# The last unit of cross-attention rows in a fused attention and expert kernel: another order of sums, residuals, keys and stores

## The reference

```
x = x + xattn(layernorm(x), ctx, ctx)      # 8 heads, queries and keys normalized per head, softmax(5 * q.k)
n = layernorm(x)
logits = n @ Wg + bg                       # 4 experts
top-2 experts of each row, softmax of their logits -> probs
for each expert i:
    the 512 rows with the highest probs of those assigned
    out[those rows] += (gelu(n[rows] @ W1[i]) @ W2[i]) * prob
x = x + out
```

## Time and profile before

| what | us |
|---|---|
| median of 3 runs (lowest to highest) | 597.75 (597.01 to 599.29) |
| the profiled execution, its own time | 598.06 |
| span of its profile | 596.2 |
| PE busy in the span | 567.0 (95%) |
| DVE busy | 342.2 (57%) |
| ACT busy | 292.4 (49%) |
| POOL busy | 184.5 (31%) |

### The profile page before, as it was taken

One profiled execution on the slowest core, in us unless ns is written; L12 is line 12 of the kernel. 1 busy time (PEld: TensorE's weight loads), 2 busy tenths in 40 slices (PEclk: granted clock), 3 DMA queues, 4 the chain that ended last, 5 costly groups with the idle time before them and its releaser, 6 DMA issues.

```text
span 596.2 us, 8893 instructions
## 1 busy us (share of the span) xinstructions
PE 567.0 (95%) x2933; PEld 403.8 (68%) x2936; DVE 342.2 (57%) x682; ACT 292.4 (49%) x451; POOL 184.5 (31%) x146
## 2 busy tenths in 40 slices
PE   8999999999997558999999999999999999999995
PEld 4445555545544325888888888888888888888884
DVE  5779999999979683534355434355534255424212
ACT  3989888788885323333334333334333334333320
POOL 8466565565632425000401500401500401500002
PEclk9999999999998859999999999999999999999998
DMA  4523433433222224422522542522542522542001
GB/s 157 195 74 124 142 110 108 142 107 107 91 90 89 100 95 141 123 90 71 187 97 88 186 149 70 180 100 86 169 168 70 181 101 81 172 170 70 1 0 71
DMA packets 49004, 67.91 MB, mean 114 GB/s; under 512 B 10960, under 2 KB 27472, under 8 KB 48976
## 3 DMA queue, kind: packets, MB, share of 16 engines
q1 hardware_dynamic: 45136, 54.97, 28.2%
q0 software_dynamic: 3840, 12.59, 6.3%
HBM read 54.77 MB, written 12.64 MB: 113 GB/s over the span
## 4 chain that ended last, share of the span: by engine, by line
PE 80%; DVE 6%; issue 5%; ACT 3%; POOL 3%; DMA 1%; POOLq 0%; DVEq 0%; ACTq 0%; SPq 0%
PE two L1541 29%; PE four L1576 10%; PE four L1574 10%; PE four L1575 10%; PE two L1364 6%; PE four L1354 5%; PE two L1379 2%; POOL rnorm L526 2%; PE four L1406 1%; PE bank_t L1399 1%; DVE junk L1126 1%; PE bank_m L1326 1%; PE bank_t L1333 1%; DVE half_sum L928 1%; PE bank_m L1341 1%
## 5 line engine op out<-in xcount | busy, mean ns | idle before, releaser
L824 ACT ACTIVATE h_f<-two 128x512 f32<-128x512 f32 x64 | 38.3, 598 | 218.8 <-PE two L1541 218.8
L1294 DVE TENSOR_TENSOR h_lo<-h_f,h_hi 128x512 fp32r<-128x512 f32 x62 | 42.7, 689 | 110.7 <-ACT h_hi L825 110.7
L1541 PE MATMUL two<-xt_hi,w_hi 128*128 (+1 forms) x256 | 101.3, 396 | 0.7 <-issue 0.7
L1541 PE MATMUL two<-xt_hi,w_lo 128*128 (+1 forms) x256 | 99.9, 390 | 0.0
L1541 PE MATMUL two<-xt_lo,w_hi 128*128 (+1 forms) x256 | 99.2, 389 | 0.0
L1576 PE MATMUL four<-w_hi,h_lo 128*128 128x512 f32 x248 | 96.5, 389 | 0.0
L1574 PE MATMUL four<-w_hi,h_hi 128*128 128x512 f32 x248 | 96.5, 389 | 0.0
L1575 PE MATMUL four<-w_lo,h_hi 128*128 128x512 f32 x248 | 96.5, 389 | 0.0
L714 ACT ACTIVATE prob<-four,rnorm 128x512 f32<-128x512 f32 x128 | 77.8, 704 | 18.3 <-POOL rnorm L526 15.1
L1263 DVE TENSOR_TENSOR w_lo<-raw,w_hi 128x2048 fp32r<-128x2048 f32 x30 | 68.7, 2290 | 23.4 <-ACT w_hi L747 23.4
L526 POOL TENSOR_TENSOR rnorm<-ss_max,power 128x8 f32<-128x8 f32 x32 | 59.2, 1851 | 42.4 <-DVE ss_max L877 28.0
(11 more groups left out here) (195 smaller groups left out, 772.2 us busy)
## 6 DMA issues: line engine op xcount, KB each, us to landing
raw<-in_L_ffn_W SPq DMA_DIRECT2D x64, 512.0 KB, 4.3
x_all<-in_x SPq DMA_DIRECT2D x16, 256.0 KB, 2.9
c_sb<-in_ctx SPq DMA_DIRECT2D x16, 256.0 KB, 3.2
out<-x_all SPq DMA_DIRECT2D x16, 256.0 KB, 2.4
x2n_dram<-x2n SPq DMA_DIRECT2D x16, 256.0 KB, 3.0
p_inv<-inv_dram SPq DMA_DIRECT2D x30, 128.0 KB, 2.9
few<-p_sum SPq DMA_DIRECT2D x60, 2.0 KB, 1.8
cst<-in_consts SPq DMA_DIRECT2D x1, 423.5 KB, 4.7
```

Of the source, the lines that this page charges most:

```text
L824: nc.scalar.activation(h_f[m % 2][:, :], z_ps[m % 2][:, :], ACT.Gelu)
L1294: nc.vector.tensor_tensor(h_lo[n][:, :], h_f[m % 2][:, :], h_hi[n][:, :].bitcast(F32), ALU.subtract).then_inc(h_split, 1)
L1541: return nc.tensor.matmul(z[:, :], w_part[c][:, w], x_k, start=start, stop=stop)
```

## The change

It does the following.

- SP: behind unit 12, unit 14's few sums are taken right behind unit 13's inverse; the stores of unit 12's and 13's x2 and x2n come behind them, three of these four also behind unit 14's inverse.
- VectorE, last unit: both pairs of half sums come before the inversion of unit 14's few sums; the first pair comes before the normalization of unit 12; the statistics of unit 13 come last. Behind `invert_sums`: residual 14 (from GpSimd), logits 12, x2n 13, statistics 14, residual 15, statistics 15, x2n 14, logits 13, x2n 15, then the first 12 units' keys, logits 14 and 15, the last keys and their copy, and only then the first count.
- GpSimd: no residual; the first two weight remainders wait for the last sums instead of the last x2n and come ahead of the last two `finish`.
- TensorE: in the last unit the full-width sums come in two parts, each as soon as its half sums are there, behind the transposes and ahead of the last weighted values and the router product of unit 12; behind it, other idle products, the transposes of unit 15 ahead of the router product of 14, and all keys transposed at the end, the first 12 units' in three parts.
- ScalarE: the rows of 14 and 15 are taken before the keys, unit 15's into a new tile `x2n_last`; the copy of the first keys is three copies of four units.

```diff
@@ sync @@
-            for u in ((end - 1, 0), (end - 1, 1), (end, 0)):
-                pass_unit(u, 3, None, None)
+            pass_unit((end - 1, 0), 3, None, None)
+            take_few((end - 1, 1))
+            store_x2n((end - 2, 1))
+            spread_inverse((end - 1, 1))
+            take_few((end, 0))
+            store_x2((end - 1, 0))
+            spread_inverse((end, 0))
+            store_x2n((end - 1, 0))
+            store_x2((end - 1, 1))
             store_x2n((end - 1, 1))
             for u in ((end, 0), (end, 1)):
                 store_x2(u)
@@ gpsimd @@
-            residual((UNITS // 2 - 1, 0))
+            pool.wait_ge(sums_ready, UNITS)
+            for q in range(2):
+                first_low(0, q)
             finish((UNITS // 2 - 1, 0))
             finish((UNITS // 2 - 1, 1))
-            pool.wait_ge(x2n_done, UNITS)
-            for q in range(2):
-                first_low(0, q)
-            pool.wait_ge(key_done, 2)
+            pool.wait_ge(late_keys, 1)
             first_low(0, 2)
@@ scalar @@
             take_x2t((UNITS // 2 - 2, 1))
-
-
+            take_x2t((UNITS // 2 - 1, 0), bank_m)
+            take_x2t((UNITS // 2 - 1, 1), rows=x2n_last)
             act.wait_ge(key_set, 1)
-            nc.scalar.activation(key_w[:, 0:EARLY, :, :], key[:, 0:EARLY, :].unsqueeze(3)
-                                 .broadcast_to([P, EARLY, E, WAYS]), ACT.Copy).then_inc(key_done, 1)
-            take_x2t((UNITS // 2 - 1, 0), bank_m)
-            take_x2t((UNITS // 2 - 1, 1))
+            for t in range(0, EARLY, 4):
+                nc.scalar.activation(key_w[:, t:t + 4, :, :], key[:, t:t + 4, :].unsqueeze(3)
+                                     .broadcast_to([P, 4, E, WAYS]), ACT.Copy).then_inc(key_done, 1)
...
-            act.wait_ge(key_t, 1)
+            act.wait_ge(key_t, 2)
             count_signs(0)
@@ vector, unit @@
-                if behind > 2:
+                if behind > 2 and ahead:
                     normalize_x2(before(before(before(u))), behind > 4)
-                if not ahead:
-                    residual(before(before(u)))
-                    statistics_x2(before(before(u)))
...
                 for h in range(2):
                     half_sums(u, 0, h, behind > 0)
-                if behind:
+                if not ahead:
+                    normalize_x2(before(before(before(u))), True)
+                    residual(before(before(u)))
+                if behind and ahead:
                     invert_few(before(u))
...
-                if not ahead:
-                    normalize_x2(before(before(u)), True)
                 for h in range(2):
                     half_sums(u, 1, h, behind > 0)
                 if not ahead:
-                    dve.wait_ge(logit_done, EARLY)
-                    keys_of(0, EARLY)
-                if behind > 2:
+                    invert_few(before(u))
+                if behind > 2 and ahead:
                     take_logits(before(before(before(u))))
-                if behind > 1 and ahead:
-                    residual(before(before(u)))
+                if behind > 1:
+                    if ahead:
+                        residual(before(before(u)))
                     statistics_x2(before(before(u)))
@@ vector, behind the units @@
             invert_sums(end)
+            residual(before(end))
+            take_logits(before(before(before(end))))
+            normalize_x2(before(before(end)), True)
             statistics_x2(before(end))
             residual(end, 1)
+            statistics_x2(end)
             normalize_x2(before(end), True)
             take_logits(before(before(end)))
-            statistics_x2(end)
             normalize_x2(end, True)
+            dve.wait_ge(logit_done, EARLY)
+            keys_of(0, EARLY)
             take_logits(before(end), bank_m)
+            take_logits(end)
             early = EARLY * P
-            dve.wait_ge(key_t, 1)
+            dve.wait_ge(logit_done, UNITS)
+            keys_of(EARLY, UNITS)
+            dve.wait_ge(key_set, 2)
+            nc.vector.tensor_copy(key_w[:, EARLY:, :, :], key[:, EARLY:, :].unsqueeze(3)
+                                  .broadcast_to([P, UNITS - EARLY, E, WAYS])).then_inc(late_keys, 1)
+            dve.wait_ge(key_t, 3)
             dve.wait_ge(thr_done, 1)
...
             put(nc.vector.scalar_tensor_tensor(rest0[:, :], count0[:, :], -2.0, excess[:, :], ALU.mult, ALU.add))
-            take_logits(end)
-            dve.wait_ge(logit_done, UNITS)
-            keys_of(EARLY, UNITS)
-            dve.wait_ge(key_set, 2)
-            nc.vector.tensor_copy(key_w[:, EARLY:, :, :], key[:, EARLY:, :].unsqueeze(3)
-                                  .broadcast_to([P, UNITS - EARLY, E, WAYS])).then_inc(key_done, 1)
...
-                    dve.wait_ge(key_t, 2)
+                    dve.wait_ge(key_t, 4)
@@ tensor @@
+            def last_sums(u, n):
+
+                for h in range(2):
+                    pe.wait_ge(halves_done[h], 2 * number(u) + n + 1)
+                pe.wait_ge(sum_taken, number(u))
+                for h in range(2):
+                    last = nc.tensor.matmul(o_ps[1][DH * h:DH * (h + 1), :], cst[:, C_ONES:C_ONES + DH],
+                                            half_sum[h][n][:, :], start=(n == 0), stop=(n == 1))
+                if n:
+                    last.then_inc(sums_ready, 1)
...
-                if behind > 2:
+                    if behind > 2:
+                        router_logits(before(before(before(u))))
+                    weighted_values(u, 2)
+                    weighted_values(u, 3)
+                    sums(u, behind)
+                else:
+                    last_sums(u, 0)
+                    last_sums(u, 1)
+                    weighted_values(u, 2)
+                    weighted_values(u, 3)
                     router_logits(before(before(before(u))))
-                if not ahead:
-                    sums(u, behind, ahead)
-                weighted_values(u, 2)
-                weighted_values(u, 3)
-                if ahead:
-                    sums(u, behind, ahead)
...
+            idle_products(12)
             pe.wait_ge(logit_done, UNITS - 3)
             transpose_x2(before(before(end)))
+            idle_products(3)
             router_logits(before(before(end)))
-            pe.wait_ge(exp_done, TT * UNITS)
-            transpose_keys(0, EARLY, 1)
             idle_products(6)
             transpose_x2(before(end), bank_m)
-            idle_products(3)
-            router_logits(before(end), bank_m)
             pe.wait_ge(logit_done, UNITS - 2)
             transpose_x2(end)
-            idle_products(3)
-            router_logits(end)
-            idle_products(10)
-            transpose_keys(EARLY, UNITS, 2)
+            router_logits(before(end), bank_m)
+            router_logits(end, rows=x2n_last)
+            pe.wait_ge(exp_done, TT * UNITS)
+            transpose_keys(0, 4, key_done, 1)
+            transpose_keys(4, 8, key_done, 2)
+            transpose_keys(8, EARLY, key_done, 3)
+            idle_products(2)
+            transpose_keys(EARLY, UNITS, late_keys)
```

More of the change, by code:

```diff
@@ L322, in xattn_moe_kernel @@
         key_done = sem("key_done")
+        late_keys = sem("late_keys")
         key_t = sem("key_t")
@@ L553, in key_remainders @@
                 pool.wait_ge(k_split, n + 1)
-            def residual(u):
-                n = number(u)
-                xu = x_all[:, bass.ds(n, 1), :].rearrange("p a d -> p (a d)")
-                pool.wait_ge(o_taken, n + 1)
-                pool.wait_ge(inv_in, 32 * (n + 1))
-                pool.wait_ge(q_split, UNITS)
-                nc.gpsimd.tensor_tensor(q_f[:, :], o_sb[u[1]][:, :], p_inv[u[1]][:, :], ALU.mult).then_inc(on_done, 1)
-                pool.wait_ge(on_done, n + 1)
-                nc.gpsimd.tensor_tensor(xu, xu, q_f[:, :], ALU.add).then_inc(x2_done, 1)
             def finish(u):
@@ L1366, in weighted_values, with sums @@
                 last.then_inc(pv_done, 1)
-            def sums(u, behind, ahead):
+            def sums(u, behind):
                 for h in range(2):
@@ L1393, in transpose_x2, with router_logits @@
                 last.then_inc(x2t_ready, 1)
-            def router_logits(u, bank=bank_t):
+            def router_logits(u, bank=bank_t, rows=x2n_t):
                 pe.wait_ge(x2t_taken, number(u) + 1)
                 for k in range(KD):
-                    last = nc.tensor.matmul(bank[:, 0:E], x2n_t[:, k, :], wg[:, k, :],
+                    last = nc.tensor.matmul(bank[:, 0:E], rows[:, k, :], wg[:, k, :],
                                             start=(k == 0), stop=(k == KD - 1))
```

21 lines of the change are left out of this document (9 added, 12 removed).

## The result

Over 20 executions of each, the changed kernel took a median of 598.91 us (597.30 to 600.59) against 597.86 us before. The ratio is 1.0023, with a 95% interval of 1.0014 to 1.0031: slower by 0.2%, which is 1.4 us by the ratio and 1.05 us by the two medians. The forecast was 595.6 with a range up to 598.2; the result lies 0.7 above the range. The profiled execution took 599.17 us (span 597.4).

The account below looks back on a forecast made before the run. Bound: the engine-hopping chain from the last exponential to the first search count, 22.44 us. The steps move that count from 202.31 to 200.15, gaining 2.15 us: 597.75 becomes 595.6, range 593.9 to 598.2.

Parts of the forecast that it names:

- Steps 1 to 3: Last unit: half sums 2.5 us less delayed, two-part sums ready 4.85 us earlier at full clock, reciprocal starting at 182.8.
- Step 4: Residual 14 moved to VectorE: its inverse lands from DRAM at 186.8, exposing a wait of 0.6 us.
- rival B: TensorE's clock falls in the last units' row work: 1.1 us slower than before, 598.9; chance 0.13.
- rival A: Unit 14's inverse becomes the bound, landing 0.9 us later than taken: gain 1.3 us, 596.5; chance 0.17.
- Steps 5 and 6: VectorE's row work ends its last statistics at 192.45; GpSimd's power takes 0.97, last x2n runs 193.5 to 194.0.
- Step 7: First keys (2.7 us, 194.0 to 196.7) cover unit 15's transposes and router products; last keys end at 198.7.
- Step 8: Three key copies, late transposes covered by VectorE's first count (0.83 us); last first-round count starts at 200.15.
- rival C: Shorter power, earlier inverse, find stage nearer a clock rise: gain 3.2 us, 594.6; same lottery can cost 1.3; chance 0.18.
- the late rise: In the find stage, TensorE's clock rising late takes up to 1.3 us back, half of about 2.9 us.

Follow-up runs that it names:

- e12: The changed kernel, unedited, run once more for its profile; 598.14 us (one execution).
- e10: Changed kernel with TensorE's first 10 idle products replaced by 6 and 30 tiny ones (52 more instructions); 597.02 us, 0.9994 of the kernel before.
- e11: e9 plus the 52 early TensorE instructions of e10; 595.99 us, 0.9972 of the kernel before.
- e14: e9 with 12 tiny idle products in place of one wide one at TensorE's start (22 more instructions); 595.39 us, 0.9967 of the kernel before.
- e2: Changed kernel with SP's queue order as before the change; 598.81 us, 1.0020 of the kernel before.
- e5: Changed kernel with the edits of e1, e3 and e4 together; 598.02 us, 1.0004 of the kernel before.
- e1: Changed kernel with the store of unit 12's x2 moved behind unit 14's inverse in SP's queue; 597.90 us, 1.0007 of the kernel before.
- e4: Changed kernel with GpSimd's third weight remainder directly behind the first two; 598.28 us, 1.0014 of the kernel before.
- e8: Changed kernel with residual 14 back on GpSimd, behind its two weight remainders; 600.66 us, 1.0052 of the kernel before.
- e3: Changed kernel with 22 idle products instead of 12 ahead of unit 13's transposes; 597.63 us, 1.0002 of the kernel before.
- e6: Changed kernel with the edits of e3 and e4, without the moved store; 598.33 us, 1.0007 of the kernel before.
- e9: e5 plus six more idle products in TensorE's tail, around the last units' transposes and router products; 596.93 us, 0.9987 of the kernel before.

## Why the prediction was wrong

- **Steps 1 to 3 held.** Half sums at once, sums in two parts at full clock, reciprocal at 2.65 behind the last exponential (forecast 2.9).
- **Step 4 failed, in the wait for the inverse.** It bounded the broadcasts' landing (2.7 to 4.0) but took the write ahead of them at the 1.4 of one row, and left out its own spread in the kernel before, 1.4 to 3.0. The write took 2.69, and the wait was 2.05 instead of 0.6. What made it late is a code transfer on the way of the write: nine packets wait until it has ended, e12 repeats it, and in e10, e11 and e14, which only add instructions at TensorE's start, it lies elsewhere and the write takes 1.4. The reasoning on the queue's stores, half of that step, was about something that showed no effect (e2, e5).
- **The forecast left the lower clock out of its sum, and rival B, which has it, was what happened.** It was given 0.13, because B put TensorE's gap at 0.9 us; it was 2.27. "0.9, or 1.8 with rival A" had A and B as separate cases. Here they are one: the late inverse makes the gap. In the six profiles of the changed kernel and its variants with a gap of 1.9 us or more (after, e1, e2, e4, e8, e12) the clock fell within 2.3 us of its end; in the seven where the gap was bridged or only 0.81 (e3, e5, e6, e9, e10, e11, e14) it held to 197 or longer. Their chances belonged together.
- **That B's price fits, 598.9 forecast and 598.9 measured, is luck.** B charges 3.3 us beyond the forecast to the clock alone, for everything TensorE does for unit 15. Measured, the count is 3.1 us behind the forecast, but from three sources: 0.8 by the last x2n (the late inverse), 1.9 by the logits behind it (the clock) and 0.3 behind them, where the 0.5 of `rest` lies. The clock rose again at 198.2, ahead of unit 15's router product (1.03) and of the last transposes (0.66).
- **Steps 5 and 6 held in length:** from the o_norm of 14 to the last x2n 6.4 us against 6.7 (193.5 - 186.8); the power took 0.80 us, between its two rows.
- **Step 7 held as long as the clock did.** With it at 1.00 (e3, e6, e14) the logits come 3.4 to 3.5 us behind the last x2n, covered but for 0.05 to 0.15 us by the first keys. At the lower clock they came at 5.2.
- **Step 8 missed a collision.** GpSimd's third remainder, tied to the late keys, now falls on `rest` (0.5 us). The prediction followed the remainders' two first pieces and not the third's new place, though the diff moves its wait.
- **The sum was right for what it described.** With the three mended, the count starts at 19.84 (e6, e14) against 20.28, and nearly all of the 0.4 is there at the last x2n (13.3 against 13.6). e14 takes 595.4 against the 595.6 forecast for the change. But e14 has more idle products and another start, and without them the clock holds only in some executions (e3, e6). The change was costed without its neighbours.
- **The stage behind the count is not of one length.** From the count to the first expert product twelve profiles take 30.8 to 31.2 us, and e3, e6, e9 and e10 take 31.4 to 31.7. The prediction had this in rival C; its "about 2.9 us more at the lower level" stands in no row, and the range's upper end, 598.2, is 0.4 above what A and the late rise give (596.5 + 1.3).
- The median of the changed kernel is not fully told by one profile. e12 is the same kernel, took 598.14 with the same late write, and had the lower clock in two shorter stretches, about 192 to 195.5 and 199 to 202, with the count at 22.6.

What stays open: why the code transfer lay at 177.4 in e3 and e6 and at 182.2 in e5, which has the same instructions for TensorE, and at 179.5 in e1, which has those of the changed kernel (182.5 and 182.2 in its two profiles). Each variant has one profile, the changed kernel two, so how often the write is late in its other executions is not known, nor how much of e1's gain over the changed kernel is that. For the same reason the shift's effect on the place of the transfer rests on three profiles with it (e10, e11, e14) against ten without.

## What to carry to other kernels

When a wait is brought onto the path by making the work beside it shorter, take its whole round trip at the slow end of its rows, not the typical one: before the change this inverse had 0.9 us to spare (two operations of 1.27 from 187.23 end at 189.8, the reciprocal that VectorE was on at 190.7), afterwards none. Price what the stall does to TensorE's clock in the same case as the stall, and check with the windows that a filled gap has not only pushed the lower clock to the next quiet stretch. And read the instruction queues among the transfers: in three of three profiles here a few small instructions at the start went with a code transfer that had left the small write that everything waits for.

## What was not expected of the hardware

- The 4 KB write of unit 14 to DRAM lands in 1.40 us, or in 2.7 to 3.0 when a 16 KB code transfer (0.9 to 1.2 us) starts 0.6 to 0.7 us behind its issue; so in 7 of 7 profiles, and in none of the 9 others for this unit. It is not the only thing that delays such a write: of the 240 writes of the inverses in the 16 profiles 56 took over 2 us, and beside 18 of these no q8 packet lay.
- An operation of VectorE on 128x1 with two SBUF inputs takes 0.66 us instead of 0.16 while GpSimd works on a 128x512 one beside it; it ends when that one ends. A count over PSUM beside the same operation was not held.
- Executions of one kernel differ by their granted clock. The 8 executions of e14 lie within 0.8 us and have 0.984 to 0.986; the 19 of the kernel before beside them lie within 4.8, the five at 0.983 with a median of 596.3, the eight at 0.981 with 598.1, the one at 0.975 at 600.95. In the 20 of the changed kernel it goes from 0.974 (600.59) to 0.980 (597.4). Where in the execution the lower clock lay is known for the profiled ones alone, and that it is the whole of the spread is not shown.
